# Experts' tiles of a mixture-of-experts layer: TensorE's program as a loop of four tiles, with rings of four buffers

## The reference

```python
logits = xt @ Wr + br                       # 8 experts
top_p, top_idx = jax.lax.top_k(softmax(logits), 2)
weights = top_p / top_p.sum(axis=-1, keepdims=True)
xe = xn[None] * ln_g[:, None] + ln_b[:, None]
h = gelu(xe @ W1 + b1)                      # 128 -> 512, exact gelu
y = h @ W2 + b2                             # 512 -> 128
out = (weights[:, :, None] * y_of_the_two_chosen).sum(axis=1)
```

## Time and profile before

| what | value |
|---|---|
| time, median of 3 runs | 1002.8 us (1002.54 to 1003.63) |
| profiled execution, span from first to last instruction (its only own time) | 1045.3 us |
| PE busy | 761.2 us, 73% |
| DVE busy | 729.2 us, 70% |
| ACT busy | 641.5 us, 61% |
| POOL busy | 587.3 us, 56% |
| granted TensorE clock, mean | 0.882 |
| instruction queue q8, whole span | 24 packets, 0.39 MB |

### The profile page before, as it was taken

One profiled execution on the slowest core, in us unless ns is written; L12 is line 12 of the kernel. 1 busy time (PEld: TensorE's weight loads), 2 busy tenths in 40 slices (PEclk: granted clock), 3 DMA queues, 4 the chain that ended last, 5 costly groups with the idle time before them and its releaser, 6 DMA issues. The chain is left out here.

```text
span 1045.3 us, 24181 instructions
## 1 busy us (share of the span) xinstructions
PE 761.2 (73%) x7837; PEld 473.6 (45%) x7837; DVE 729.2 (70%) x1821; ACT 641.5 (61%) x1446; POOL 587.3 (56%) x760
## 2 busy tenths in 40 slices
PE   2857888888888888888888599665554306899960
PEld 2444444444454454444544244212443305777750
DVE  2585788888888888888887715697745543666646
ACT  2656888887888888888888332285322404777740
POOL 0045777767767767767767499200065561555560
PEclk8896999999999999999999699888655557999995
DMA  9009999980000000000000050130011112222317
GB/s 218 1 2 203 172 187 118 6 3 0 0 0 0 0 0 0 0 0 0 0 0 0 4 159 1 55 126 3 1 41 41 33 44 60 64 83 73 83 47 241
DMA packets 109052, 54.07 MB, mean 52 GB/s; under 512 B 42688, under 2 KB 100824, under 8 KB 109008
## 3 DMA queue, kind: packets, MB, share of 16 engines
q1 hardware_dynamic: 102624, 43.34, 27.5%
q0 software_dynamic: 4544, 9.38, 2.8%
q10 hardware_dynamic: 1840, 0.79, 0.4%
HBM read 21.49 MB, written 29.44 MB: 49 GB/s over the span
## 5 line engine op out<-in xcount | busy, mean ns | idle before, releaser
L534 DVE SCALAR_TENSOR_TENSOR l_m<-l_m,l_eta,lp_g 128x256 f32<-128x256 f32 x512 | 219.6, 476 | 39.5 <-PE lp_g L646 26.0
L383 POOL TENSOR_TENSOR s_w<-l_kw,l_m 128x512 f32<-128x512 f32 x192 | 238.4, 1278 | 12.0 <-DVE l_m L534 12.0
L480 ACT ACTIVATE l_kw<-s_w,l_keep_lr 128x256 f32<-128x256 f32 x384 | 171.3, 507 | 0.0
L1338 POOL DMA_INDIRECT f_yg<-f_yr,f_xmeta x78 | 78.7, 1009 | 75.1 <-DVE f_yr L1668 55.9
L1333 POOL DMA_INDIRECT f_xg<-f_xrow,f_place x64 | 62.9, 983 | 74.7 <-DVE f_place L1564 56.4
L1313 ACT ACTIVATE f_hh<-fp_v,f_bcol 128x256 f32<-128x256 f32 x156 | 63.2, 480 | 33.4 <-PE fp_v L1433 32.4
L473 ACT COPY l_wt<-lp_b 128x512 f32<-128x512 f32 x96 | 56.4, 588 | 27.8 <-PE lp_b L639 27.8
L388 POOL TENSOR_TENSOR l_kw<-s_w,l_keep 128x512 f32<-128x512 f32 x64 | 65.2, 1040 | 0.0
L639 PE MATMUL lp_b<-s_cst,s_w 128*128 128x128 f32 x384 | 62.7, 287 | 2.3 <-ACT s_w L521 1.3
L1433 PE MATMUL fp_v<-f_xf,s_w_hi 128*128 128x256 bf16 x312 | 56.0, 281 | 9.3 <-DVE f_xmeta L1648 7.2
L639 PEld LDWEIGHTS lp_b<-s_cst,s_w 128*128 128x128 f32 x384 | 43.7, 143 | 32.5 <-ACT l_wt L473 13.8
(11 more groups left out here) (323 smaller groups left out, 2016.4 us busy)
## 6 DMA issues: line engine op xcount, KB each, us to landing
f_xg<-s_pad SPq DMA_DIRECT2D x1, 17280.0 KB, 106.7
f_xt<-f_xg SPq DMA_DIRECT2D x39, 130.0 KB
r_w<-in_L_ffn_W_dram SPq DMA_DIRECT2D x16, 256.0 KB, 3.1
s_w<-f_yg SPq DMA_DIRECT2D x16, 256.0 KB, 3.7
xs<-in_x_dram SPq DMA_DIRECT2D x8, 256.0 KB, 7.5
t_w<-in_L_ffn_W_dram SPq DMA_DIRECT2D x8, 256.0 KB
out_dram<-s_x SPq DMA_DIRECT2D x8, 256.0 KB, 3.0
s_xsh<-s_xl SPq DMA_DIRECT2D x4, 448.0 KB, 3.5
```

What stands on the lines that cost most here:

```text
L383: nc.gpsimd.tensor_tensor(W[k][:, half(h), :], KW[k][:, half(h), :], M[k][:, half(h), :], ALU.add).then_inc(w_ready[k], 1)
L480: m = nc.scalar.mul(KW[k][:, b, :], W[k][:, b, :], keep_lr[:, b:b + 1])
L534: i = nc.vector.scalar_tensor_tensor(out=M[k][:, b, :], in0=M[k][:, b, :], scalar=eta[:, b:b + 1], in1=ps_g[b][:, 0:256], op0=ALU.mult, op ...
L1338: nc.gpsimd.indirect_dma_start(sb["yg"][:, :], bass.IndirectOffsetOnAxis(ap=xmeta[:, j, a, 0:1].bitcast(mybir.dt.int32), axis=0), yr[j % R ...
```

## The change

The rings of token, result and hidden-unit buffers get four places instead of three; the third and fourth `hs` pair and all result buffers lie in the left-over memory. TensorE's order of turn, first layer and second layer stays, but of its 41 steps the first 6 are written out, the next 32 are a hardware loop of 8 rounds with four steps each, and the last 3 are written out again. In the loop, semaphore counts and the addresses of `owner_i` and `mine` are expressions of the loop's register r (`at(r, k)` is 4r + k). The expert's number is not kept: it is loaded before the first layer and again before the second, in all steps. ScalarE's and VectorE's code is put in the same form, but is still written out (`plain`). VectorE's wait before the remainders asks for the second layer of tile j - 4 instead of j - 3. Core of the diff:

```diff
-    RING = 3
+    RING = 4
+    AHEAD, ROUNDS = 6, 8
...
-        hs.append([spare[:, 512 * i:512 * i + 512].bitcast(BF16).rearrange("p (h n) -> p h n", h=NH) for i in range(2)])
-        yr = [buf(f"yr{i}", [128, 2, 128]) for i in range(RING)]
+        for n in range(2):
+            hs.append([spare[:, 1024 * n + 512 * i:1024 * n + 512 * i + 512].bitcast(BF16).rearrange("p (h n) -> p h n", h=NH) for i in range(2)])
+        yr = [spare[:, 2048 + 256 * i:2304 + 256 * i].rearrange("p (a n) -> p a n", a=2) for i in range(RING)]
...
+        def at(r, k, n=1):
+            return r * (RING // n) + k // n
+
+        def rounds(engine, step, last):
+            for k in range(AHEAD):
+                step(0, k)
+            with engine.Fori(0, ROUNDS) as r:
+                for k in range(RING):
+                    step(r, AHEAD + k)
+            for k in range(AHEAD, last - RING * ROUNDS):
+                step(ROUNDS, k)
+
+        def plain(step, last):
+            for k in range(last):
+                step(0, k)
...
-                def owner_of(j):
-                    return nc.tensor.value_load(owner_i[0:1, j:j + 1], min_val=0, max_val=E - 1)
-                owners = {}
+                def owner_of(r, k):
+                    return nc.tensor.value_load(owner_i[0:1, bass.ds(at(r, k), 1)], min_val=0, max_val=E - 1)
+
+                def first_layer(r, k, e):
+                    pe.wait_ge(xf_ready, 2 * at(r, k) + 2)
+                    if k >= 2:
+                        pe.wait_ge(h_ready, NH * at(r, k - 1))
+                    ...
+                def second_layer(r, k, e):
+                    pe.wait_ge(h_lo, 2 * at(r, k) + 2)
+                    if k == 1:
+                        pe.wait_ge(owner_ready, 4)
+                    if k >= 2:
+                        pe.wait_ge(y_ready, at(r, k - 1))
+                    ...
+                def layers(r, k):
+                    if RING * ROUNDS * (r is ROUNDS) + k + 1 < NJ:
+                        turn(r, k + 1)
+                    if RING * ROUNDS * (r is ROUNDS) + k < NJ:
+                        first_layer(r, k, owner_of(r, k))
+                    if k >= 2:
+                        second_layer(r, k - 2, owner_of(r, k - 2))
...
-                turn(0)
-                for j in range(NJ + 2):
-                    ...
+                turn(0, 0)
+                rounds(pe, layers, NJ + 2)
...
+                def remainders(r, k):
+                    if k >= 4:
+                        dve.wait_ge(y_done, at(r, k - 3))
+                    ...
+                def summed(r, k):
+                    dve.wait_ge(y_done, at(r, k) + 1)
+                    if k >= RING:
+                        dve.wait_ge(yr_free[k % RING], 32 * at(r, k, RING))
+                    ...
+                arrive(0, 0)
+                plain(passed, NJ + 2)
```

More of the change, by code:

```diff
@@ L1306, in _, with activated @@
                 act.wait_ge(owner_ready, 4)
-                for j in range(NJ):
-                    if j >= 2:
-                        act.wait_ge(h_lo, 2 * (j - 1))
+                def activated(r, k):
+                    if k >= 2:
+                        act.wait_ge(h_lo, 2 * at(r, k - 1))
                     for h in range(NH):
                         if h % 2 == 0:
[L1312 to L1316, removed]
+                            act.wait_ge(h_done, 2 * at(r, k) + h // 2 + 1)
+                        nc.scalar.activation(hh[k % 2][:, h, :], ps_h[k % 2][:, SL * h:SL * h + SL], ACT.Gelu,
+                                             bias=bcol[:, h, bass.ds(at(r, k), 1)]).then_inc(h_ready, 1)
+                    if k >= 3:
+                        act.wait_ge(y_done, at(r, k - 2))
                     for p in range(2):
-                        act.wait_ge(h_ready, NH * j + 2 * p + 2)
-                        nc.scalar.copy(hs[j % 3][0][:, 2 * p:2 * p + 2, :], hh[j % 2][:, 2 * p:2 * p + 2, :]).then_inc(h_hi, 1)
+                        act.wait_ge(h_ready, NH * at(r, k) + 2 * p + 2)
+                        nc.scalar.copy(hs[k % RING][0][:, 2 * p:2 * p + 2, :], hh[k % 2][:, 2 * p:2 * p + 2, :]).then_inc(h_hi, 1)
+                plain(activated, NJ)
             @block.gpsimd
@@ L1398, in _, with turn @@
                     counts(g)
[L1400 to L1404, removed]
+                def turn(r, k):
+                    pe.wait_ge(xt_in[k % RING], 16 * at(r, k, RING) + 16)
+                    if k >= 2:
+                        pe.wait_ge(xf_ready, 2 * at(r, k - 1))
                     for i in range(4):
-                        m = nc.tensor.transpose(ps_xb[j % 2][:, 128 * i:128 * i + 128], xt[j % RING][:, i % 2, 128 * (i // 2):128 * (i // 2) + 128], identb[:, :])
+                        m = nc.tensor.transpose(ps_xb[k % 2][:, 128 * i:128 * i + 128], xt[k % RING][:, i % 2, 128 * (i // 2):128 * (i // 2) + 128], identb[:, :])
                     m.then_inc(xt_turned, 1)
@@ L1410, in chosen @@
                     return w[:, bass.ds(e, 1), 128 * h:128 * h + 128].rearrange("p a n -> p (a n)")
-                def owner_of(j):
-                    return nc.tensor.value_load(owner_i[0:1, j:j + 1], min_val=0, max_val=E - 1)
-                owners = {}
+                def owner_of(r, k):
[4 more added lines that the diff above has]
+                        pe.wait_ge(h_ready, NH * at(r, k - 1))
+                    for h in range(NH):
+                        p = ps_h[k % 2][:, SL * h:SL * h + SL]
+                        for n, (b, c) in enumerate(PRODUCTS):
+                            m = nc.tensor.matmul(p, chosen(w1s[b], e, h), xf[k % 2][:, c, :], start=n == 0, stop=n == 2)
+                        if h % 2 == 1:
+                            m.then_inc(h_done, 1)
@@ new lines, in second_layer @@
+                def second_layer(r, k, e):
+                    pe.wait_ge(h_lo, 2 * at(r, k) + 2)
+                    if k == 1:
+                        pe.wait_ge(owner_ready, 4)
+                    if k >= 2:
+                        pe.wait_ge(y_ready, at(r, k - 1))
+                    for h in range(NH):
+                        w = w2b[:, bass.ds(e, 1), h, :, :].rearrange("p a c n -> p (a c n)")
+                        for a in range(2):
+                            p = ps_y[k % 2][:, 256 * a:256 * a + 256]
+                            nc.tensor.matmul(p, hs[k % RING][0][:, h, 128 * a:128 * a + 128], w, start=(a, h) == (0, 0), stop=False)
+                            nc.tensor.matmul(p[:, 0:128], hs[k % RING][1][:, h, 128 * a:128 * a + 128], w[:, 0:128], start=False, stop=False)
+                    m = nc.tensor.matmul(ps_y[k % 2].rearrange("p (a n) -> p a n", a=2)[:, :, 0:128], mine[:, bass.ds(at(r, k), 1)].to_broadcast([128, 128]),
+                                         btab[:, H:H + 128].rearrange("p (a n) -> p a n", a=1).to_broadcast([128, 2, 128]), start=False, stop=True)
+                    m.then_inc(y_done, 1)
@@ L1640, in _ @@
                 nc.vector.tensor_copy(bcol[:, :, :], ps_o).then_inc(owner_ready, 1)
[L1642 to L1668, removed]
+                def arrive(r, k):
+                    dve.wait_ge(xt_turned, at(r, k) + 1)
+                    if k >= 2:
+                        dve.wait_ge(h_done, 2 * at(r, k - 1))
+                    nc.vector.tensor_copy(xf[k % 2][:, :, :].rearrange("p a n -> p (a n)"), ps_xb[k % 2][:, 0:512]).then_inc(xf_ready, 1)
+                    nc.vector.tensor_copy(xmeta[:, bass.ds(at(r, k), 1), :, :].rearrange("p j a c -> p (j a) c"), tile[k % RING][:, :, 128:130]).then_inc(xf_ready, 1)
@@ new lines, in remainders @@
+                def remainders(r, k):
+                    if k >= 4:
+                        dve.wait_ge(y_done, at(r, k - 3))
+                    for p in range(2):
+                        dve.wait_ge(h_hi, 2 * at(r, k) + p + 1)
+                        nc.vector.tensor_tensor(hs[k % RING][1][:, 2 * p:2 * p + 2, :], hh[k % 2][:, 2 * p:2 * p + 2, :],
+                                                hs[k % RING][0][:, 2 * p:2 * p + 2, :], ALU.subtract).then_inc(h_lo, 1)
+                def summed(r, k):
+                    dve.wait_ge(y_done, at(r, k) + 1)
+                    if k >= RING:
+                        dve.wait_ge(yr_free[k % RING], 32 * at(r, k, RING))
+                    dve.wait_ge(xf_ready, 2 * at(r, k) + 2)
+                    parts = ps_y[k % 2].rearrange("p (a c n) -> p a c n", a=2, c=2)
+                    nc.vector.tensor_reduce(yr[k % RING][:, :, :], parts.rearrange("p a c n -> p a n c"), AX.X, ALU.add).then_inc(y_ready, 1)
@@ L1669, in _, with passed @@
+                def passed(r, k):
+                    if RING * ROUNDS * (r is ROUNDS) + k + 1 < NJ:
+                        arrive(r, k + 1)
+                    if RING * ROUNDS * (r is ROUNDS) + k < NJ:
+                        remainders(r, k)
+                    if k >= 2:
+                        summed(r, k - 2)
+                arrive(0, 0)
+                plain(passed, NJ + 2)
```

## The result

The changed kernel takes 1029.21 us, the median of 4 runs (1027.87 to 1031.18), against 1003.21 us of the kernel before in the same runs (1002.54 to 1004.98). The ratio is 1.0248 with a 95% interval of 1.0224 to 1.0272: 26.0 us slower. The forecast was 1012 us with a range of 991 to 1023. The direction was right; the time lies above the range.

The account below looks back on a forecast made before the run. It took TensorE at 3.50 us a tile, held-back marks included, as today's pace and its sequencer at 3.72 as the new bound: 7.0 + 0.9 + 1.5 = +9.4 us, scaled by 0.96 to +9.0, 1012 us, range 991 to 1023.

Parts of the forecast that it names:

- What bounds the kernel now: Expert stage: 3.50 us a tile, 2.97 undisturbed plus 0.53 for TensorE's held-back marks; its sequencer has 0.45 us slack.
- Fetches as the likely cause of the held marks: TensorE's instruction fetches, 13 packets for 39 tiles, likely hold its marks; removing them is worth at most 17 us.
- Recording slows the run: Profiled span 1045.3 us, 42.5 above the median, put down to recording; the difference was scaled by 0.96.
- The sequencer as the new bound, 3.72 us a tile: TensorE's serial sequencer work in the loop, 2.5 + 0.6 + 0.52 + 0.10 us a tile: +7.0 us; chance 0.51.
- The values and the back edge: Loop's register values, 26 a round at 0.08 us, +0.52 us a tile; addition, branch and counter reload +0.10.
- The argument from the place of the load: The second load, +0.6 us, stands between a tile's two layers, where only the first layer's last few matmuls are queued.
- First pass of the body, 1.5 us: The loop body must still be fetched once, about one and a half blocks: +1.5 us.
- Rings, 0: Four token, result and hidden-unit buffers instead of three: 0 us each.
- Tail unchanged: The part of the kernel behind 1007 us is unchanged.
- Rival A: Fetches were the whole loss, sequencer under 3.36 us a tile: faster, 989 us at full effect, 996 at 3.2; chance 0.30.
- rival B: Gain and cost cancel, sequencer at 3.36 to 3.49 us a tile: within 2 us of 1003; chance 0.12.
- rival C: The loop body is fetched again each round, 8 x 2.7 = 22 us on top: 1033 us; chance 0.07.

Follow-up runs that it names:

- experiment 1: The kernel before, unchanged, recorded again: 1002.98 us, ratio 0.9994, recording span 1001.8 us.
- experiment 9: The changed kernel with four loads of the expert's number a round instead of eight, kept in four registers over the back edge, without bounds check: 1002.64 us, ratio 0.998.
- experiment 2: The kernel before, unrolled with rings of three, with only the second load of the expert's number added: 1013.35 us, ratio 1.0099.
- experiment 3: The changed kernel with TensorE's program written out instead of looped; second load and rings of four stay: 1014.44 us, ratio 1.0111.
- Experiment 6: The kernel before with the second load added ahead of the first layer, right behind the first load: 1012.91 us, ratio 1.0096.
- experiment 5: The changed kernel with TensorE's program written out and each expert's number kept, so no second load; rings of four stay: 1004.37 us, ratio 0.9994.
- experiment 8: The changed kernel with one load a round bringing six numbers into six registers, numbers kept in the written-out steps: 1010.89 us, ratio 1.0076.
- experiment 10: The changed kernel with a round's six numbers brought by two loads, of four and of two numbers: 1003.51 us, ratio 0.9986.
- experiment 7: The kernel before with a second load of the expert's number in every second tile only: 1005.84 us, ratio 1.0029.

## Why the prediction was wrong, step by step

- *What bounds the kernel now*: **this is the step that failed.** "3.50 us a tile", made of 2.97 and 0.53 for one disturbance in three tiles, was right for the recording and wrong for the kernel: 2.96 us (experiment 1). The sum took the 0.53 as something the change would remove, and so the loop's 32 tiles were credited with 17 us in all that the timed kernel never lost: 32 x (3.72 - 3.50) = 7.0 us in the sum should have been 32 x (3.72 - 2.96) = 24.3.
- *Fetches as the likely cause of the held marks*: wrong as a cost. 13 packets go with 2.96 us a tile in the kernel before, and 4 with 2.96 in experiment 9. The Trainium skill ("Runtime: NRT & Kernel Launch", section Instruction fetch mechanics) says that crossing a block is mostly hidden; experiment 1 agrees. Whether the fetches held the marks in the one disturbed recording stays open; that both came once in three tiles is all that speaks for it, and the stretches without a packet in experiment 1 speak against a fetch under way.
- *"Recording slows the run"*: the warning read as a habit. The span stood 42.5 us above the timed median. In the other thirteen recordings the span is 1.8 to 2.2 us *below* the time it was taken with. That one number said that the recording was not of an ordinary execution, and the scaling by 0.96 kept the disturbed base.
- *The sequencer as the new bound, 3.72 us a tile*: right, 3.717 measured. But its parts were off in both directions, and that they cancel is luck. The load group takes 0.65 and the rest 2.59, 0.14 more than the 0.6 and 2.5 of the sum (experiment 2). The values and the back edge cost 0.49, where 0.62 was charged (experiment 3), with 25 operations against 26 counted. One of these takes some 0.10 us with its gap, not 0.08, and the back edge 0.5 us a round, not 0.41; what the sum left out is that six of the twelve waits of four tiles, 0.1 us each, no longer stand there (experiment 3). Worked out from these rows, 23 x 0.10 + 0.5 - 0.6 = 2.2 us a round, an estimate of 0.55 a tile.
- *The argument from the place of the load*: not needed. Experiment 6 moves it, and nothing changes.
- *First pass of the body, 1.5 us*: too high. The first round takes 15.45 us (868.58 to 884.03) and the second 15.14, against 14.87 later: 0.85 us in all. That this is the fetching of the body is not shown.
- *Rings, 0*: right (experiment 5). *Tail unchanged*: right. *Rival A* fell with its condition, a sequencer under 3.36 us a tile; *rival B* likewise; *rival C* by the 4 packets.

With the base put right the forecast's own terms give 24.3 + 1.0 for the seven tiles outside (3.1 - 2.96 each) + 1.5 = +26.8, or 1030.0 us on 1003.2. With the measured parts it is 24.3, seven tiles outside at 0.27 = 1.9, and 0.85 for the first rounds: +27.1, or 1030.3. Measured are 1029.21, about 1 us less than either sum. From the first tile's first layer to the last one's, the recordings say nearly the same: 848.60 to 987.74 us after, 848.16 to 961.38 in experiment 1, so 139.1 against 113.2, +25.9.

## What to carry to other kernels

Before a loss is read from a recording, set its span beside the timed median: a span 42 us above it, with waits that end by "remote", means that the tiles' length must be taken from an undisturbed stretch (here 2.97 us, and it stood there) or from a second recording. When TensorE's matmuls are short, add up its sequencer's steps in a tile and compare the sum with the array's time; here 2.5 of 2.96 us were already used, so a second load of a number (0.65 us) cost 10 us in 39 tiles and a hardware loop as first written 15 more. A loop is not slow in itself: with four loads a round, carried in registers and without their checks, it ran in the unrolled program's time, and so it did with two loads for six numbers; but the serial work has to be spread, not only small in the mean.

## What the runs showed of the hardware that was not expected

- The array's pace in a tile is exact to its pieces. In the chain matmuls follow one another by 0.109 or 0.056 us, and 12 x 0.109 + 4 x 0.056 + 8 x (0.109 + 0.056) + 0.109 = 2.96 us, the whole tile. So in this stage of the kernel before the array's matmuls stand back to back.
- Loading a number into a register of TensorE's sequencer lasts 0.30 us for one and 0.83 to 0.98 for six (experiment 8), but 0.34 to 0.36 for the four and 0.53 to 0.55 for the two of experiment 10, so no price for each further one comes out. The Trainium skill (the same page and section) gives about 200 ns a register even in bulk. It says so of loads from device memory, and the numbers here lie in the core's buffers, so this is no test of it.
- The sequencer's excess in one tile is made good in the next as far as the queued matmuls reach (0.27 us over in experiment 7: mostly hidden), but 1.7 us in a row are not (experiment 8: 0.6 us lost a round).
- A loop whose body holds four tiles, some 380 instructions by the prediction's count, is fetched once: 4 packets in the whole stage, and its branch takes 0.21 us. The Trainium skill's rule (same page and section) that a taken branch out of the current two pages must fetch first does not show here; how many pages the body covers no row tells, so this is no test of the rule either.
- Identical programs can leave recordings 43.5 us apart, with waits for marks of up to 12.2 us that end by "remote". What does it is open.
